# Third pass of a graph network: node features loaded by quarters from packed rows, node chunks stored from ScalarE's queue

## The reference

```python
h = jnp.maximum(_layernorm(x, axis=-1), 0.0)
x = x + L0(h)     # agg = segment_sum(h[src] + edge_feats, dst); relu(agg @ W1 + b1) @ W2 + b2; batch norm
h = jnp.maximum(_layernorm(x, axis=-1), 0.0)
x = x + L1(h)     # twice: relu(segment_sum((h @ W)[src] * enorm, dst) + b); then a norm over all
```

## Time and profile before

| | us |
|---|---|
| median of 3 runs | 2736.61 (2732.78 to 2737.0) |
| the profiled execution | 2731.35 |
| its span, first to last instruction | 2730.0 |
| PE busy | 2450.0 (90%) |
| GpSimd (POOL) busy | 1920.0 (70%) |
| VectorE (DVE) busy | 1509.8 (55%) |
| ScalarE (ACT) busy | 1323.0 (48%) |
| mean granted TensorE clock | 0.972 of full |

### The profile page before, as it was taken

How to read it: one execution, slowest core, us unless ns; L and a number is a source line. 1 busy time by engine, 2 the same in 40 slices (tenths; PEclk the granted TensorE clock), 3 DMA queues, 4 the chain that set the end, 5 groups by cost and what they waited for, 6 DMA issues and landing times.

```text
span 2730.0 us, 67333 instructions
## 1 busy us (share of the span) xinstructions
PE 2450.0 (90%) x26318; PEld 2369.3 (87%) x26318; DVE 1509.8 (55%) x3805; ACT 1323.0 (48%) x3271; POOL 1920.0 (70%) x1833
## 2 busy tenths in 40 slices
PE   1399899999999999965999999999969999999996
PEld 0298899888898889855999999999969999999996
DVE  8898899888898889844333433333302222222212
ACT  8588788888888888855432433423200000000001
POOL 5777877777777777702777777777437777777772
PEclk9999999999999999967999999999979999999998
DMA  4566566666566666636566565665676666565654
GB/s 111 134 179 175 168 178 175 169 187 177 162 184 179 184 170 175 176 113 206 196 230 201 186 221 191 198 219 180 216 194 211 209 216 214 198 205 190 211 197 140
DMA packets 339567, 506.63 MB, mean 186 GB/s; under 512 B 277602, under 2 KB 283160, under 8 KB 313905
## 3 DMA queue, kind: packets, MB, share of 16 engines
q1 hardware_dynamic: 270454, 292.79, 34.4%
q0 software_dynamic: 57952, 89.89, 14.7%
q10 hardware_dynamic: 10840, 119.53, 11.6%
HBM read 364.94 MB, written 137.13 MB: 184 GB/s over the span
## 4 chain that ended last, share of the span: by engine, by line
PE 55%; POOL 19%; DVE 8%; issue 7%; ACT 6%; DMA 4%; SPq 1%; DVEq 0%; ACTq 0%; POOLq 0%
PE psum L1118 38%; POOL arena L1297 19%; PE psum L1098 5%; PE psum L1140 4%; PE psum L1133 3%; DMA arena<-in_edge_attr_dram 3%; ACT arena L1230 2%; DVE arena L964 2%; ACT arena L1217 1%; PE psum L1076 1%; DVE arena L990 1%; PE psum L1153 1%; DMA arena<-table,srcT 1%; PE psum L1156 1%; SPq L1312 1%
## 5 line engine op out<-in xcount | busy, mean ns | idle before, releaser
L1297 POOL DMA_INDIRECT arena<-table,srcT x1770 | 1839.9, 1040 | 650.2 <-issue 606.6
L1118 PE MATMUL psum<-arena 125*125 125x193 bf16 (+1 forms) x19600 | 1974.5, 247 | 44.4 <-DMA arena<-counts 22.9
L1118 PEld LDWEIGHTS psum<-arena 125*125 125x125 fp8e4 x19600 | 1860.1, 137 | 53.3 <-DMA arena<-counts 23.3
L1230 ACT ACTIVATE arena<-psum 125x500 uint16<-125x500 f32 (+1 forms) x923 | 662.9, 718 | 436.1 <-PE psum L1098 431.8
L1217 ACT ACTIVATE arena<-iota,modT 128x125 uint8<-128x125 f16 x1775 | 602.9, 391 | 2.1 <-ACT arena L1230 2.1
L964 DVE TENSOR_SCALAR arena<-iota,keyT,oddT 128x300 f16<-128x300 f16 x1775 | 575.7, 357 | 22.3 <-PE psum L1098 18.8
L1098 PE MATMUL psum<-arena 128*125 128x300 f16 x1775 | 524.2, 297 | 54.5 <-ACT arena L1230 34.1
L1279 ACT ACTIVATE cneg<-cst 125x1 f32<-125x1 f32 x25 | 5.1, 203 | 689.3 <-DVE arena L1051 689.3
L1098 PEld LDWEIGHTS psum<-arena 128*125 128x125 fp8e4 x1775 | 243.4, 137 | 100.2 <-DVE arena L964 70.8
L974 DVE SCALAR_TENSOR_TENSOR arena<-relT,psum 128x960 bf16<-128x960 f16 x272 | 308.9, 1136 | 0.0
L990 DVE TENSOR_TENSOR arena<-arena 128x650 f32<-128x650 f32 x334 | 273.0, 817 | 14.2 <-DMA arena<-in_edge_attr_dram 13.9
(11 more groups left out here) (222 smaller groups left out, 1014.1 us busy)
## 6 DMA issues: line engine op xcount, KB each, us to landing
arena<-counts SPq DMA_DIRECT2D x125, 1600.0 KB
counts<-arena ACTq DMA_DIRECT2D x71, 1600.0 KB
arena<-in_edge_attr_dram SPq DMA_DIRECT2D x166, 320.0 KB
arena<-table,srcT POOLq DMA_INDIRECT x1770
table<-arena SPq DMA_DIRECT2D x8, 1050.0 KB
table<-arena SPq DMA_DIRECT2D x25, 168.0 KB
arena<-table SPq DMA_DIRECT2D x4, 1050.0 KB
arena<-in_x_dram ACTq DMA_DIRECT2D x4, 700.0 KB
```

Source lines behind the costliest of these rows:

```text
L1118: last = pe.matmul(ps_v[n % 2][0:PN, 0:xc], A(slot)[0:PN, j, 0:PN], Xs[0:PN, j, 0:xc], start=(j == 0), stop=(j == J - 1))
L1230: act.activation(A2(slot)[0:PN, :, i // 2 * NWORD:i // 2 * NWORD + n_w], ps_b[at % NBANK][0:PN, 0:n_w * J].rearrange("p (x j) -> p j x", j=J),
L1297: pool.indirect_dma_start(out=gbuf(slot)[0:parts, t, :], out_offset=None, in_=tables[k], in_offset=bass.IndirectOffsetOnAxis(ap=idx, axis= ...
```

## The change

1. "tstore" moves from SP's list to ScalarE's, at the same due time (8.6 behind "node"). It waits for VectorE's `v_nlo` there and issues the same two DMAs.
2. The third pass reads its features through `Xt`, the same memory with rows of 192 numbers, so that a partition's quarter is one run of 9600 bytes in DRAM and in SBUF.
3. The loads are due in the last dense tile of the second pass, in the order 0, 1, 3, 2. Quarters 0 and 1 wait only until that tile's matmuls have passed the rows that they overwrite (`p_past`, set behind matmul 28 and 52 of 100); quarters 3 and 2 wait for the end of the tile (`p_app`). All still wait for the stores that they read.
4. The first tile of the third pass takes its places in that order of quarters.

```diff
+X_ORDER = (0, 1, 3, 2)
...
-    t, stores = -100.0, []
+    t = -100.0
...
                 dve.append((t + 7.6, "nlo", i))
-                sp.append((t + 8.6, "tstore", i))
-                stores.append(t + 8.6)
+                act.append((t + 8.6, "tstore", i))
...
     if k == 1:
-        for q in range(NCH):
-            j0, j1 = q * J // NCH, (q + 1) * J // NCH
-            s = max(stores[i] for i, (u, c) in enumerate(done) if c * JH < j1 and (c + 1) * JH > j0)
-            sp.append((max(total, s) + 0.3 + 0.1 * q, "xload", q))
+        for i, q in enumerate(X_ORDER):
+            sp.append((start[D - 1] + 6 * (i + 1) + 1.5, "xload", q))
...
         Xs = arena[:, 0:o_A].bitcast(BF16).rearrange("p (j x) -> p j x", x=XC)
+        Xt = arena[:, 0:J * 3 * F // 2].bitcast(BF16).rearrange("p (j x) -> p j x", x=3 * F)
...
+            X = Xs if k < 2 else Xt
+            past = [((c + 1) * JC + AP_STEP - 1) // AP_STEP - 1 for c in range(NCH - 1)]
...
-                    for j in range(i * AP_STEP, (i + 1) * AP_STEP):
+                    for at in range(i * AP_STEP, (i + 1) * AP_STEP):
+                        j = at
                         if k == 1 and q == 0 and j % JC == 0:
                             pe.wait_ge(v_lo, NCH + j // JC + 1)
-                        if k == 2 and q == 0 and j % JC == 0:
-                            pe.wait_ge(d_xs[j // JC], NBAND * 16)
-                        last = pe.matmul(ps_v[n % 2][0:PN, 0:xc], A(slot)[0:PN, j, 0:PN], Xs[0:PN, j, 0:xc],
-                                         start=(j == 0), stop=(j == J - 1))
+                        if k == 2 and q == 0:
+                            j = X_ORDER[at // JC] * JC + at % JC
+                            if at % JC == 0:
+                                pe.wait_ge(d_xs[j // JC], NBAND * 16)
+                        last = pe.matmul(ps_v[n % 2][0:PN, 0:xc], A(slot)[0:PN, j, 0:PN], X[0:PN, j, 0:xc],
+                                         start=(at == 0), stop=(at == J - 1))
                     if i == NAP - 1:
                         last.then_inc(p_app, 1)
+                    elif k == 1 and q == D1 - 1 and i in past:
+                        last.then_inc(p_past, 1)
...
+                elif kind == "tstore":
+                    c = pl["done"][v][1]
+                    act.wait_ge(v_nlo, v + 1)
+                    for p0, p1 in bands():
+                        act.dma_start(tables[2].rearrange("(p j) f -> p j f", p=PN)[p0:p1, c * JH:(c + 1) * JH, :],
+                                      node_x(v % 2)[p0:p1]).then_inc(st_node[v % 2], 16)
...
                 elif kind == "xload":
                     j0, j1 = chunk[v]
-                    sp.wait_ge(p_app, plans[2]["d0"])
+                    if v in X_ORDER[NCH - 2:]:
+                        sp.wait_ge(p_app, plans[2]["d0"])
+                    else:
+                        sp.wait_ge(p_past, v + 1)
...
-                    sp_xs(2, v, d_xs[v])
+                    for p0, p1 in bands():
+                        sp.dma_start(Xt[p0:p1, j0:j1, :],
+                                     tables[2].rearrange("(p j) f -> p j f", p=PN)[p0:p1, j0:j1, :]).then_inc(d_xs[v], 16)
```

More of the change, by code:

```diff
@@ L416, in bass_gnn_preln_kernel @@
         st_node = [sem(f"st_node{i}") for i in range(2)]
+        p_past = sem("p_past")
         d_xs = [sem(f"d_xs{i}") for i in range(NCH)]
```

## The result

| | kernel before | changed kernel |
|---|---|---|
| median of 7 runs, us | 2736.61 (2730.38 to 2740.02) | 2722.56 (2715.64 to 2726.41) |
| ratio, 95% interval | 1 | 0.995 (0.9934 to 0.9965) |
| the profiled execution, us | 2731.35 | 2723.48 |

A forecast was written before the change was run, and what follows sets the result against it. The prediction took GpSimd's unbroken gather stream to bound the third pass, so only its 12.4 us earlier start counted, with PE's 19.6 us otherwise turning into waits: median 2736.61 less 12.4 gives 2724.2 us, range 2717 to 2731.

The forecast's parts named there:

- The third pass is bound by the gathers: Third pass: GpSimd's 532 gathers run 663.8 us without being held up, so its end depends on when GpSimd starts.
- GpSimd starts 12.4 us earlier: Behind the second pass: last store issued 11.0 us earlier from ScalarE, landing in 4.1 us; gathers from 2004.6 (11.0 to 13.7).
- PE is 19.6 us earlier: Third pass's first tile: with loads by quarters it ends at 2013.7 against 2033.3 (15.4 to 24.8).
- Quarter 3 at 1993.8: SP's queue at the end of the second pass: quarter 3's load goes out at 1993.8 and has landed by 2003.3.
- Rival 2: Behind the second pass: last store lands late, after the bulk loads; gathers start at 2008.8, -8.2 us, 2728.4; chance 0.12.
- Group 0's lead becomes 18 us: Third pass: PE's first edge group trails its gathers by 18 us instead of 25.2, used up after some 14 groups, not 24.
- Packed rows bring nothing: Third-pass matmuls: rows of 192 instead of 194 numbers save nothing, bounds 0 and 3.6 ns a matmul.
- ScalarE's hold costs nothing: Second pass: stores hold ScalarE 0.77 to 1.2 us, within 2.16 us of eviction slack; cost nothing, bounds 0 and 4 us.
- Rival 3: Second pass, evictions at L1230: ScalarE's hold behind stores stalls the builds; 2744.2 us at 2.96 us each; chance 0.05.
- The sum: Whole kernel: last groups run 12.4 us earlier, PE's further 7 us become waits, nothing changes behind group 52; 2724.2 us.
- The prediction's own sign of being wrong: Whole kernel: the forecast is wrong if the difference at the end is not that of GpSimd's start; no size given.
- Rival 1: Third pass: PE's gain goes through whole if gathers can catch up; end moves by 19.6 us, to 2717.0; chance 0.08.

The follow-up runs named there:

- e7: Changed kernel with nine instead of ten gathers in each group of the third pass, the tenth matmul reading what the slot held before; one run, 2688.21 us.
- e9: Changed kernel with the third pass's edge groups spread later and GpSimd's flag read ahead of its wait for the stores; four runs, 2710.94 us, 0.9912 of the kernel before.
- e6: Changed kernel with 24 small iotas on GpSimd ahead of the third pass's gathers; slow chips, 4206.54 and 4215.41 us (kernel before 4212.1 and 4214.97).
- e4: Changed kernel without early loads: quarters 0 and 1 too wait for the end of the second pass's last tile; one run, 2730.23 us.
- e2: Changed kernel with the node chunk stores kept on SP, each in its planned place; slow chips, 0.9967 and 0.9975 of the kernel before.
- e3: Changed kernel with the third pass reading rows of 194 numbers as before, loads in pieces of 384 bytes; one run, 2730.61 us.
- e1: Kernel before with only the node chunk stores moved to ScalarE's queue, loads as before; slow chips, 0.9982 and 1.0011 of the kernel before.

## Why the prediction was right

**The median came out at 2722.56, forecast 2724.2**, range 2717 to 2731. Step by step:

- *The third pass is bound by the gathers.* Right, and shown by e7 and e9. The stream's length (663.7 to 663.8 us) is the same in the five traces with all gathers on the chips of full pace. The one run that would have delayed GpSimd alone (e6) could not tell.
- *GpSimd starts 12.4 us earlier.* Measured 13.3. The last store's issue was forecast at +5.7 and came at +6.3 (the chain ahead of it took 0.6 us longer), its landing at 4.1 us behind it and took 2.6.
- *Why it took only 2.6 us* the prediction did not see. First gather behind the last store's issue: 6.5 us before, 3.6 changed, 8.5 with wide rows, 12.1 without early loads, 10.5 store alone, 9.5 loads alone. In the changed kernel only the end of quarter 1's load and of the last but one store was still in flight (both complete at +8.4), and the DMA engines were busy 35%; no new load had been issued, because SP stood at the wait for the last but one store until +8.4. In e4, with three loads in flight, they were busy 80% while the last store took 11.0 us:

```profile
2005.70:2016.74 11.04, 6.81 (x52) 6.36 (x53) 0.00 (x0) 0.00 (x0) 0.00 (x0) 0.71 0.80 215
```

- *That was luck.* With quarter 3 out at +0, as forecast, the store would have shared the engines with it, as in e2, where quarter 3 went out at +4.3 and the store took 8.4 us. Landing in 8.4 instead of 2.6 us would put the first gather at about +15.7, 5.8 us later, and the time near 2728 (an estimate): the forecast's 4.1 us was reached with quarter 3's load in flight, and held only because it was not.
- *PE is 19.6 us earlier.* Measured 14.1, the step that failed. "Quarter 3 at 1993.8" (+0) was +8.4. Rival 2's mechanism, a store held up by bulk loads, struck one store earlier than I had put it: the early loads of quarters 0 and 1 (2.4 MB) kept the store of the chunk that quarter 3 needs for 12.5 us. I had priced every load's landing, and no landing of that store. A tile of counts was in flight too, but it landed at -2.2, and in e4 the same fetch stood beside a store that took 3.0 us.
- *Group 0's lead becomes 18 us.* It is 24.6, as PE came 5.5 us later than forecast and the gathers 0.9 earlier. First wait at group 19, not 14; waits 23.2 us in sum, not 26. The 14 was a slip in the sum: 7.2 us less lead at 0.89 us a group are 8 groups fewer than 24, so 16. With a lead of 24.6 that rule gives 23, and it was 19 because the packed rows quicken PE: (2266.69 - 1.88 - 2048.28) / 19 = 11.40 us a group instead of 11.59, so the lead shrinks by 1.08 a group.
- *Packed rows bring nothing.* Wrong in size: 1.10 ns a matmul, inside the bounds given (0 to 3.6). The gathered rows' 84 ns that I took it from are from other matmuls (96 columns of weights in bf16). As said there, most of it hides behind the gathers: it is 7.6 us of PE on 6900 matmuls. What is not hidden stands behind the last long wait, group 46: to the last fold 95.5 us before and 93.6 after. 960 matmuls by 1.10 ns are 1.1 us of these 1.9. This also splits the two pairs of kernels that e3 and e4 left open: the last fold is 688.7 and 689.2 us behind the first gather with wide rows (before, e3), 686.5 and 686.8 with packed ones (changed, e4). Within a pair it follows the first gather within 0.5 us.
- *ScalarE's hold costs nothing.* The second pass, from its first to its last fold, is 713.6 before and 714.4 to 714.9 in the five traces with the stores on ScalarE: 0.8 to 1.3 us longer, with one trace of before. Rival 3 is out.
- *The sum.* -13.3 for the first gather and -2.2 behind it make the 15.5 us of the two profiles, and the second pass gives 0.8 back: 14.7, against 13.7 (9.6 to 18) by the ratio. The forecast of -12.4 had the first term 0.9 and the second 2.2 us too small, with nothing for the 0.8. The prediction's own sign of being wrong, that the difference at the end is not that of GpSimd's start, holds for these 2.2 us: about half of them are the packed rows, by the estimate above. Rival 1 (-19.6) was out for the reason given: PE's time is not what the end waits for.

The Trainium skill (DMA: Bandwidth & Descriptors, section Issuing engines are not separate DMA queues) says that DMAs started by different engines run on the same 16 DMA engines and interleave, and that another issuing engine only saves sequencer time, usually little beside the transfer. These traces agree, but for the "little". What the other queue saved is sequencer time, here 11 us of strided issues, and the loads alone save it as well (e2). And the stores do share the engines: the last one took 2.6 us with the engines busy 35%, and 7.4 to 11.0 us beside loads just issued (e3, e2, e1, e4).

## What to carry to other kernels

An engine that is busy 70% can be the bound: look for a stream that never pauses for another engine, check the slack of its users over time, and ask what releases its first instruction. Price a small transfer that many wait for by what is in flight at its issue, and hold bulk loads back until it has landed; in this kernel a wait that nobody had planned for it did that; a version that does it on purpose was not run. Work that doesn't need the slow stream belongs ahead of its last results: moving 14 us of it there (e9) gained 11.6 us between the medians, where the whole change had gained 14.05.

## What was not expected of the hardware

- A store of 188 KB (168 + 19.5 by partition band) took from 2.2 us (e7) to 12.5 us (changed kernel) from issue to landing, by what was in flight.
- Two DMAs of a strided quarter: 112 partitions take 0.6 to 0.8 us of SP's queue, the other 13 partitions with 325 pieces 2.8 to 6.1 us. Packed, either takes 0.3 to 0.7.
- With rows of 384 bytes a 125 x 192 bf16 matmul follows the one before it by 82.5 ns, with rows of 388 bytes by 83.6.
- Two chips on which PE issues at times one matmul in 2.8 us, and all kernels take 4.2 ms.
